# Two groups of four transposes merged into one, ahead of a product's last piece, in a state-space and channel-mixing block

## What is computed

```
h = layernorm(x) * (1 + ca) + sa
x = x + ga * ssm(h)        # u, gate = W_in h; decay, b_t from u; h_t = d*h + (1-d)*b; y = W_C h
                           # z = y * silu(gate) + h * D;  W_out z
h = layernorm(x) * (1 + cb) + sb
x = x + gb * ffn(h)        # xr, xk = mixes of h and of h one token earlier
                           # sigmoid(xr @ W_r) * (relu(xk @ W_k)**2 @ W_v)
```

## Time and profile before

| | us |
|---|---|
| median of 3 runs | 377.53 |
| lowest, highest | 377.43, 378.26 |
| the profiled execution, its own time | 377.79 |
| its span in the trace | 375.90 |

### The profile page before, as it was taken

The page is one execution under the profiler, slowest core; times in us unless marked ns, Lnnn a source line. Parts: engine busy times, 40 slices in busy tenths (PEclk is TensorE's granted clock), DMA queues, the critical chain, the costliest instruction groups (busy, mean ns, idle before and its releaser), DMA issues.

```text
span 375.9 us, 5636 instructions
## 1 busy us (share of the span) xinstructions
PE 359.1 (96%) x1708; PEld 276.4 (74%) x1711; DVE 302.0 (80%) x637; ACT 308.8 (82%) x419; POOL 265.6 (71%) x274
## 2 busy tenths in 40 slices
PE   7999799999999999999999999999999999999773
PEld 4776477777778787777778777777778777776551
DVE  2788967988889797988989797988979787678452
ACT  4466779899898989899898989899898989886571
POOL 2073558969686878969686878969686876948552
PEclk9999999999999999999999999999999999999998
DMA  8931111130403131130403131130303030100011
GB/s 281 395 103 56 56 58 56 60 111 0 145 24 112 58 112 56 60 111 2 143 26 113 56 112 58 60 109 3 112 2 112 1 113 0 57 3 24 32 58 56
DMA packets 18607, 29.16 MB, mean 78 GB/s; under 512 B 1168, under 2 KB 9616, under 8 KB 18448
## 3 DMA queue, kind: packets, MB, share of 16 engines
q1 hardware_dynamic: 18144, 28.71, 22.1%
q10 hardware_dynamic: 432, 0.09, 0.1%
HBM read 20.40 MB, written 8.39 MB: 77 GB/s over the span
## 4 chain that ended last, share of the span: by engine, by line
POOL 47%; issue 39%; PE 5%; DVE 3%; ACT 2%; DMA 1%; POOLq 1%; DVEq 0%; SPq 0%; ACTq 0%
POOL xr_lo L730 11%; POOL z_lo L787 7%; POOL xk_lo L730 6%; POOL k_lo L730 6%; POOL h_lo L730 6%; POOL state_lo L777 5%; POOL rstd L740 3%; PE slot L220 2%; DMA w_in<-weights_in 1%; PE slot L234 1%; PE slot L347 1%; DVE stats L548 1%; POOL prev L771 1%; POOL spread L738 1%; POOL spread L737 1%
## 5 line engine op out<-in xcount | busy, mean ns | idle before, releaser
L766 POOL TENSOR_TENSOR rstd<-mv,half_neg 128x4 f32<-128x4 f32 x16 | 16.1, 1007 | 53.5 <-DVE mv L561 53.5
L435 ACT ACTIVATE prev<-slot,mod,mix_prev 128x512 f32<-128x512 f32 x64 | 46.3, 786 | 1.7 <-PE slot L227 1.7
L220 PE MATMUL slot<-h_hi,wf_hi 128*128 128x512 f32 x128 | 45.9, 399 | 0.4 <-ACT h_hi L461 0.4
L220 PE MATMUL slot<-h_hi,wf_lo 128*128 128x512 f32 x128 | 45.6, 397 | 0.0
L730 POOL TENSOR_TENSOR xk_lo<-xk,xk_hi 128x512 fp32r<-128x512 f32 x32 | 40.9, 1298 | 6.6 <-ACT xk_hi L446 5.8
L787 POOL TENSOR_TENSOR z_lo<-z,z_hi 128x512 fp32r<-128x512 f32 x28 | 36.2, 1294 | 12.0 <-ACT z_hi L442 7.9
L730 POOL TENSOR_TENSOR k_lo<-k_act,k_hi 128x512 fp32r<-128x512 f32 x32 | 40.7, 1293 | 4.9 <-ACT k_act L516 4.9
L730 POOL TENSOR_TENSOR xr_lo<-xr,xr_hi 128x512 fp32r<-128x512 f32 x32 | 42.5, 1331 | 0.0
L730 POOL TENSOR_TENSOR h_lo<-h,h_hi 128x512 fp32r<-128x512 f32 x30 | 38.3, 1302 | 3.1 <-ACT h_hi L461 3.1
L227 PE MATMUL slot<-ident,xn 128*128 128x128 f32 x256 | 35.9, 274 | 2.8 <-DVE xn L585 2.1
L227 PEld LDWEIGHTS slot<-ident,xn 128*128 128x128 f32 x256 | 29.5, 141 | 11.4 <-issue 4.9
(11 more groups left out here) (121 smaller groups left out, 1002.9 us busy)
## 6 DMA issues: line engine op xcount, KB each, us to landing
x_tok<-x_tok_in SPq DMA_DIRECT2D x16, 512.0 KB, 3.5
x_ch<-x_ch_in SPq DMA_DIRECT2D x16, 512.0 KB, 3.7
x_out<-wmod SPq DMA_DIRECT2D x15, 512.0 KB, 3.0
wmod<-wmod_in SPq DMA_DIRECT2D x1, 1024.0 KB, 10.0
w_in<-weights_in SPq DMA_DIRECT2D x1, 1024.0 KB, 11.5
w_in<-weights_in SPq DMA_DIRECT2D x1, 768.0 KB, 5.5
wmod<-wmod_in SPq DMA_DIRECT2D x1, 512.0 KB, 6.4
x_out<-wmod SPq DMA_DIRECT2D x2, 256.0 KB, 2.2
```

Of the source, the lines that this page charges most:

```text
L220: ins = nc.tensor.matmul(out, w[:, c, at + d * P:at + (d + 1) * P], x[:, c, :], start=first, stop=last)
L435: return nc.scalar.activation(prev[:, mix, i, 1:T + 1], ps_n[:, i, :], ACT.Identity, bias=mod_at(SHIFT2 + i, k), scale=mix_prev[:, mix, i, ...
L766: nc.gpsimd.tensor_tensor(rstd2[:, c % 2], mv2[:, c % 2, 1, :], half_neg[:], ALU.pow).then_inc(rstd2_ok, 1)
```

## The change

TensorE transposes all four tiles of `xn2` in one group of eight, ahead of the last piece of the receptance product, where it transposed two tiles, did that piece, and transposed the other two. The two semaphores of the tiles become one, raised by VectorE after the fourth tile, and GpSimd waits for that one.

```diff
--- before.py
+++ after.py
@@ -144,7 +144,7 @@
 
         st1_ok, mv1_ok, xn1b_ok = sem("st1_ok"), sem("mv1_ok"), sem("xn1b_ok")
         st2_ok, halves2_ok, spread2_ok, mv2_ok = sem("st2_ok"), sem("halves2_ok"), sem("spread2_ok"), sem("mv2_ok")
-        xn2a_ok, xn2b_ok = sem("xn2a_ok"), sem("xn2b_ok")
+        xn2_ok = sem("xn2_ok")
         clip_ok, drive_ok, state_ok, yg_ok, rv_ok = sem("clip_ok"), sem("drive_ok"), sem("state_ok"), sem("yg_ok"), sem("rv_ok")
         z_ok, x1_ok, xk_ok, xr_ok, x2_ok = sems("z_ok"), sems("x1_ok"), sems("xk_ok"), sems("xr_ok"), sems("x2_ok")
 
@@ -220,10 +220,10 @@
                     ins = nc.tensor.matmul(out, w[:, c, at + d * P:at + (d + 1) * P], x[:, c, :], start=first, stop=last)
                 return ins
 
-            def to_channels(out, x, tiles=range(TT)):
+            def to_channels(out, x):
 
                 for c in range(CH):
-                    for t in tiles:
+                    for t in range(TT):
                         last = nc.tensor.transpose(out[:, c, t * P:(t + 1) * P], x[:, t, c * P:(c + 1) * P], ident[:])
                 return last
 
@@ -361,18 +361,15 @@
                         last = nc.tensor.matmul(ps_y[:, i, :], wy_hi[:, i * P:(i + 1) * P], state_lo[:], start=False, stop=True)
                     last.then_inc(y_ps, 1)
                 if live(c):
-                    pe.wait_ge(xn2a_ok, c + 1)
+                    pe.wait_ge(xn2_ok, c + 1)
                     if live(b):
                         pe.wait_ge(silu_ok, b + 1)
                     else:
                         pe.wait_ge(relu_ok, d + 1)
-                    to_channels(ps_n, xn2, range(0, TT // 2))
+                    to_channels(ps_n, xn2).then_inc(t3_ps, 1)
                 if live(d):
                     pe.wait_ge(xrlo_ok[1], d + 1)
                     half(r_out, wl_hi, MIX_R, xr_lo, 1, last=True).then_inc(r_ps, 1)
-                if live(c):
-                    pe.wait_ge(xn2b_ok, c + 1)
-                    to_channels(ps_n, xn2, range(TT // 2, TT)).then_inc(t3_ps, 1)
                 if live(d):
                     pe.wait_ge(khi_ok, d + 1)
                     if not live(c):
@@ -579,11 +576,11 @@
                     last = nc.vector.tensor_scalar(xn1[:, t, :], x_tok[:, k % 3, t, :], rstd1[:, k % 2, t:t + 1], shift1[:, k % 2, t:t + 1], ALU.mult, ALU.add)
                 last.then_inc(xn1b_ok, 1)
 
-            def ln2_apply(k, tiles, done):
-
-                for t in tiles:
+            def ln2_apply(k):
+
+                for t in range(TT):
                     last = nc.vector.tensor_scalar(xn2[:, t, :], ps_x1[:, t, :], mv2[:, k % 2, 0, t:t + 1], rstd2[:, k % 2, t:t + 1], ALU.subtract, ALU.mult)
-                last.then_inc(done, 1)
+                last.then_inc(xn2_ok, 1)
 
             def rest_of_modulation():
 
@@ -653,8 +650,7 @@
                 if live(c):
                     dve.wait_ge(rstd2_ok, c + 1)
                     before(dve, t3_ps, c)
-                    ln2_apply(c, range(0, TT // 2), xn2a_ok)
-                    ln2_apply(c, range(TT // 2, TT), xn2b_ok)
+                    ln2_apply(c)
                 if live(b):
                     dve.wait_ge(y_ps, b + 1)
                     dve.wait_ge(silu_ok, b + 1)
@@ -761,8 +757,7 @@
                     low_part(xr_lo[:, 0], xr[:, 0], xr_hi[:, 0], xrhi_ok[0], r_ps, xrlo_ok[0], d)
                 if live(c):
                     pool.wait_ge(mv2_ok, c + 1)
-                    before(pool, xn2a_ok, c - 1)
-                    before(pool, xn2b_ok, c - 1)
+                    before(pool, xn2_ok, c - 1)
                     nc.gpsimd.tensor_tensor(rstd2[:, c % 2], mv2[:, c % 2, 1, :], half_neg[:], ALU.pow).then_inc(rstd2_ok, 1)
                     if c == 0:
                         pool.wait_ge(mix_ok, 1)
```

## The result

The changed kernel takes 386.29 us (median of 6 runs, 385.48 to 387.49) against 377.52 before: a ratio of 1.0228, 95% interval 1.0211 to 1.0245, or 8.8 us slower (8.0 to 9.2 by that interval). The direction and the mechanism are those forecast; the time lies 0.1 us above the end of the stated range, and 1.4 above the 384.9 forecast. The profiled execution of the changed kernel took 387.49 us, the longest of the six (span 385.7).

The account below looks back on a forecast made before the run. The bound was a loop from r_ps through ScalarE to z_hi[1] and TensorE's fixed list to the next r_ps. 6.02 + 1.34 = +7.4 us on the median of 377.53 gave 384.9, range 382.4 to 386.2.

Parts of the forecast that it names:

- (a): TensorE's x2 transposes: one group of eight in place of two of four gives 0.01 us a step, put at nothing.
- (b): Receptance piece behind four more transposes: r_ps and ScalarE's chain to z_hi[1] 0.43 us later in 14 steps, 6.0 us.
- (c): t3_ps comes about 0.55 us earlier, but its only taker, `prev`, queues behind ScalarE's gate: worth nothing.
- (d): TensorE's merged wait for all four tiles is met 0.9 us early in a middle step: costs nothing.
- (e): Step s = 17, where TensorE waits for the norm: receptance pair and gate 1.34 us later, bounds 0 and 1.4.
- The signs: Expected in the changed profile: step 21.6 us, eight transposes advancing by 0.79, idle before `r_gate` 0.76, z_hi wait 0.64.
- slack on ScalarE: Rival: ScalarE's chain to z_hi[1] has slack, so only the tail's +1.34 us is paid, giving 378.7; chance 0.06.
- given back before state_hi: Rival: TensorE's 0.33 us idle before state_hi absorbs that much each step, total +2.7, giving 380.3; chance 0.07.
- gain from fewer changes of kind: Rival: pairs behind transposes save 0.08 us in 15 steps, giving 376.3, chance 0.02; or no net change, chance 0.03.

Follow-up runs that it names:

- e4: Kernel before, with both groups of four, still with two waits and two semaphores, ahead of the receptance piece; 385.64 us, ratio 1.0198.
- e8: Like e6 (receptance piece first), but with two groups of four and two semaphores; 374.81 us, ratio 0.9923.
- e6: Changed kernel with its group of eight behind the receptance piece in place of ahead of it; 374.90 us, ratio 0.9916.
- e1: Kernel before with one group of eight ahead of the receptance piece in every step but s = 17; 384.46 us, ratio 1.0169.
- e7: Changed kernel with ScalarE's first two `previous` ahead of its gate, TensorE's list untouched; 378.39 us, ratio 1.0011.
- e5: Kernel before, order kept, but the first group of four waits for all four tiles; 379.64 us, ratio 1.0043.
- e3b: Changed kernel plus matmuls of zeros in TensorE's waits: 13 before the transposes of s = 17, 10 before s = 18 and s = 19; 385.01 us.
- e2: Kernel before with one group of eight in s = 17 only, two groups of four in every other step; 380.23 us, ratio 1.0054.
- e3: Changed kernel plus 13 matmuls of zeros ahead of the wait for the four tiles in s = 17 only; 386.69 us.
- e11: Like e9, but 10 matmuls of zeros ahead of the receptance piece in s = 17, and 6 before s = 18 and s = 19; 374.68 us.
- e9: e6 plus matmuls of zeros in s = 17 (13, behind the receptance piece), s = 18 and s = 19; 378.99 us, ratio 1.0026.

## Why the prediction was right, and where it fell short

- *(a) The grouping is worth nothing.* Right: e4 has the step of the changed kernel, and e8 that of e6.
- *(b) 14 x 0.43 = 6.0 through the loop.* Right, and not by luck: +5.93 up to s = 17 in the two profiles, 0.43 a step, 5.9 in the lower runs of e1. That the loop is the cause is shown from both sides: e7 takes `r_ps` away from its head and the loss goes; e6 brings it forward and the step falls below that of before. The sign to read was the pair that advanced by 0.51 in place of 0.47, with ScalarE busy without a gap from the gate to z_hi[1]: a stall of 0.04 showed that there was no slack of 0.43. One detail was off: TensorE does not come to the z_hi[1] products at the old time, some 0.1 of the loss falls at those of z_hi[0].
- *(c) The earlier t3_ps has no taker.* Right as the lists stand; e7 gave it one.
- *(d) The wait for four tiles is met early.* Right: e5, step 21.20.
- *(e) s = 17 costs 1.34.* The wait was right (tiles at 358.77 + 1.90 = 360.67, transposes at 360.73; 1.32 with the clock held, e3b), but this term was mis-sized: the prediction wrote that "TensorE's clock stays at full" and so put what the clock costs at nothing. With the clock, the place costs 2.4 (e2), and the clock's share of the whole change is 1.6 (e3b), enough for the 1.4 by which the median passed the forecast. What could have been read beforehand: TensorE already waited 2.21 for xk, and the 1.34 would lengthen idle times, not work. In the row of the granted clock the last slice, an 8, is the one in which TensorE has run out of work. No row of the kernel before shows a product slowed by it, so the size could not be read there.
- *The signs.* The step (21.63), the spacing of the eight transposes (0.81), the idle before `r_gate` (0.77) and before `dt` (1.57) came as foreseen. The weight load of z_hi[1] waits 0.56 and 7.9 in total, not 0.64 and near 9; part of the loss falls at z_hi[0]. In s = 17 the gate comes 2.6 later against its step and waits 6.8, where 1.3 and 5.5 were foreseen: the clock again.
- *The rivals.* No slack on ScalarE, nothing given back before state_hi (its wait is 0.33 in both), no gain from fewer changes of kind.

Open stays in which place the clock falls in the executions of the change that have no trace. The profiled one lost 2.5 in both, and e3 1.5 in s = 18 alone, at medians (386.29 and 386.69) that are nearly the same. That the clock falls in one execution and not in another after the same 2.1 us idle (e1 and before) was seen, not explained.

## What to carry to other kernels

Where two engines wait for each other once per step, both are the bound, and the order inside the busier one counts beside its work: here the same work in three orders gave mean steps of 20.98, 21.19 and 21.62. Put first what starts the other engine's chain. Read such a loop from the spacing of the work behind the wait rather than from the busy share. And where a change lengthens an idle time of TensorE, price what its clock does afterwards as well as the wait; zeros held it here when they stood ahead of the wait in which TensorE is idle (e3b, e11), and cost 4 us when they stood behind it and ran at the lower clock (e9).

## What was unexpected of the hardware

- After 3.03 us idle, eight transposes took 1.97 in place of 1.05, and four 512-column matmuls after a later idle 2.61 took 1.91 in place of 1.1. With the idle times filled, four runs lay within 0.4 us (e3b); unfilled, six within 2.0.
- After 2.12 us idle the clock had fallen in one execution (e1) and, after as long, had not in another (the kernel before). In e2 it fell only some 0.8 us into the work behind the idle 3.12 (granted 1.00 from 354.8 to 355.6, 0.56 from 355.6 to 359.5).
- Filling only the first of two idle times saved nothing (e3, 386.69); in its profile the loss stands behind the second.
